# Projection stage of a cross-attention and feed-forward kernel: four re-orderings around the first two batches and the last

## The reference, cut to what matters

```python
# x, ctx: (8, 512, 512); mask: (8, 1, 512, 512); bias: (1, 16, 512, 512); 16 heads of 32
def attention(Q, K, V, mask, bias, ...):
    q = split_heads(Q @ Wq.T + bq); k = split_heads(K @ Wk.T + bk); v = split_heads(V @ Wv.T + bv)
    s = einsum('bhqd,bhkd->bhqk', q, k) / sqrt(32)
    s = where(mask == 0, -1e9, s) + bias
    return einsum('bhqk,bhkd->bhqd', softmax(s), v) @ Wo.T + bo
x = x + attention(layernorm(x), ctx, ctx, mask, bias, ...)
x = x + ffn(layernorm(x), W1, W2, ...)   # gelu(x W1^T) W2^T plus a routed low-rank part, width 2048
```

## Time and profile before

| | |
|---|---|
| median of 3 runs | 1793.49 us (1792.51 to 1795.33) |
| the profiled execution | 1790.85 us, span 1789.0 us |
| PE busy in the span | 1760.2 us (98%) |
| DVE, ACT, POOL busy | 1275.6 (71%), 912.1 (51%), 970.5 (54%) |
| mean granted TensorE clock | 0.997 of full speed |
| DMA in the first 7 of 40 slices | 330 to 356 GB/s, busy share 9 tenths or more |

### The profile page before, as it was taken

One profiled execution on the slowest core, in us unless ns is written; L12 is line 12 of the kernel. 1 busy time (PEld: TensorE's weight loads), 2 busy tenths in 40 slices (PEclk: granted clock), 3 DMA queues, 4 the chain that ended last, 5 costly groups with the idle time before them and its releaser, 6 DMA issues.

```text
span 1789.0 us, 33907 instructions
## 1 busy us (share of the span) xinstructions
PE 1760.2 (98%) x11842; PEld 1357.6 (76%) x11842; DVE 1275.6 (71%) x2866; ACT 912.1 (51%) x2038; POOL 970.5 (54%) x466
## 2 busy tenths in 40 slices
PE   8899998999999999999999999999999999999999
PEld 7788876555555555555778888888988889888888
DVE  8777788999999999999757555464654556645553
ACT  4323225999999999999434232312423224232231
POOL 1423347999999999998446343332342333423321
PEclk9999999999999999999999999999999999999999
DMA  9999999545436336340578684866948659577584
GB/s 330 330 346 341 343 356 336 180 143 189 143 99 233 113 125 226 106 131 19 171 239 301 226 291 141 317 198 188 320 131 299 208 187 320 157 263 239 163 280 144
DMA packets 213031, 396.90 MB, mean 222 GB/s; under 512 B 15232, under 2 KB 54784, under 8 KB 212352
## 3 DMA queue, kind: packets, MB, share of 16 engines
q1 hardware_dynamic: 209312, 381.62, 63.3%
q0 software_dynamic: 3264, 12.58, 2.0%
q10 hardware_dynamic: 288, 0.52, 0.1%
HBM read 319.17 MB, written 75.50 MB: 221 GB/s over the span
## 4 chain that ended last, share of the span: by engine, by line
PE 50%; DVE 2%; issue 0%; POOL 0%; ACT 0%; DVEq 0%; ACTq 0%
PE banks L2104 20%; PE banks L2078 17%; PE banks L1977 7%; PE banks L2016 5%; PE banks L1971 1%; DVE k_x L1532 0%; DVE k_x L1703 0%; DVE h_q L1693 0%; DVE n_w L1630 0%; DVE n_ru_l L1518 0%; DVE n_stats L1539 0%; DVE n_ru_l L1698 0%; DVE n_zo L1525 0%; DVE n_g_h L1710 0%; DVE n_sel L1638 0%
## 5 line engine op out<-in xcount | busy, mean ns | idle before, releaser
L2078 PEld LDWEIGHTS banks<-n_zo,n_w 128*128 128x128 f32 x2688 | 499.3, 188 | 66.8 <-DVE h_bias L1816 2.4
L2078 PE MATMUL banks<-n_zo,n_w 128*128 128x256 f32 x2688 | 532.5, 281 | 4.3 <-DVE h_bias L1816 2.2
L1461 POOL TENSOR_TENSOR n_g_l<-h_pos,n_g_h 128x512 fp32r<-128x512 f32 x128 | 196.3, 1533 | 559.4 <-DVE n_g_h L1710 559.4
L2104 PE MATMUL banks<-n_w,n_g_h 128*128 128x512 f32 x1024 | 383.2, 394 | 0.0
L1178 ACT ACTIVATE l_tiles<-l_tiles,l_small 128x512 f32<-128x512 f32 x376 | 267.4, 715 | 0.0
L1112 DVE CUSTOM_DVE_ANT_0 l_tiles<-banks,l_tiles 128x512 f32<-128x512 f32 x353 | 224.9, 687 | 24.7 <-PE banks L1014 23.9
L1025 PEld LDWEIGHTS banks<-ident,l_tiles 128*128 128x128 f32 x1524 | 164.8, 142 | 90.3 <-issue 71.8
L1025 PE MATMUL banks<-ident,l_tiles 128*128 128x128 f32 x1524 | 209.5, 281 | 0.7 <-ACT a_pT L1156 0.7
L2104 PE MATMUL banks<-n_w,n_g_l 128*128 128x512 f32 x512 | 201.7, 394 | 0.0
L2104 PEld LDWEIGHTS banks<-n_w,n_g_h 128*128 128x128 f32 x1024 | 193.0, 188 | 8.1
L1119 DVE COPY a_pT<-banks 128x512 f32<-128x512 f32 x256 | 164.6, 683 | 6.3 <-PE banks L1025 4.2
(11 more groups left out here) (263 smaller groups left out, 3523.9 us busy)
## 6 DMA issues: line engine op xcount, KB each, us to landing
n_w<-wf_d SPq DMA_DIRECT2D x448, 256.0 KB, 3.7
n_w<-w_d SPq DMA_DIRECT2D x112, 512.0 KB, 4.5
a_pos<-pos_d SPq DMA_DIRECT2D x16, 1024.0 KB, 5.6
l_bias<-in_bias POOLq DMA_DIRECT2D x9, 1024.0 KB, 7.9
l_tiles<-in_x SPq DMA_DIRECT2D x8, 1024.0 KB, 10.2
l_tiles<-in_xT SPq DMA_DIRECT2D x8, 1024.0 KB, 12.6
l_bias<-in_mask SPq DMA_DIRECT2D x8, 1024.0 KB, 14.3
k_d<-l_tiles SPq DMA_DIRECT2D x8, 1024.0 KB, 11.4
```

Of the source, the lines that this page charges most:

```text
L1461: pool.tensor_tensor(out=g_l[:, j % NG, :], in0=g_f[:, j % NG, :], in1=g_h[:, j % NG, :].bitcast(F32), op=ALU.subtract).then_inc(g_low, 1)
L2078: last = pe.matmul(bank, w1[:, q % NR, m, k * P:(k + 1) * P], zo[:, j, MOVING[i], k, :], start=s == 0 and i in (P1, P6, P5), stop=s == NPP ...
L2104: last = pe.matmul(ps_y[:, t, :], (g_h, g_l)[i][:, j % NG, t * P:(t + 1) * P], w2[:, j % NG, k, :], start=f == 0 and m == 0, stop=f == NF ...
```

## The change

Six edits, all in `project`. (1) ScalarE's first batch: the rounding of the four quarters of the value weights and the four key copies alternate, instead of four and four. (2) ScalarE: the rounding of the first W1 slice, `feed_high(0)`, leaves the end of batch 0 and stands in batch 1 behind `keep_row(1)`; the other slices stay where they were. (3) TensorE: from batch 1 on `R_HIGH` stands behind V0 instead of before it and `R_LOW` behind V1 instead of behind V0. (4) VectorE: from batch 1 on the first value addition is made behind the second diagonal, ahead of the mask, instead of with the other three. (5) VectorE, last batch: the order of scaling, masking and minima. (6) SP, last batch: values are stored by tiles, and one bias load goes between the second and the third.

```diff
@@ SP, body
+                for t in range(0 if more else NT):
+                    sp.wait_ge(bank_free, NPB + NVQ * b + t + 1)
+                    sp.dma_start(tokens(v_d[b])[:, t, :], v_s[:, t, :]).then_inc(v_out, 16)
+                    if t == 1:
+                        sp.wait_ge(min_done, B)
+                        sp.wait_ge(pos_out, 16 * (B + 1))
+                        load_bias(3)
@@ VectorE, body
                 diagonal(r_l)
+                if b > 0:
+                    values(b, 0, 1)
...
                 if b > 0:
-                    values(b, 0, NT)
+                    values(b, 1, NT)
...
+                else:
+                    scale_queries(b, 0)
+                    mask_queries(b, 0)
+                    first_minima(0)
+                    scale_queries(b, 1)
+                    scale_queries(b, 2)
+                    first_minima(1)
+                    mask_queries(b, 1)
+                    mask_queries(b, 2)
+                    scale_queries(b, 3)
+                    mask_queries(b, 3)
@@ ScalarE
+            def feed_high(b):
+                act.wait_ge(wf_in, 32 * (b + 1))
+                act.wait_ge(wf_out, 32 * (b + 1))
+                act.wait_ge(wo_out, 32)
+                for n, (ops, raw) in enumerate(f_parts):
+                    if n == 2:
+                        act.wait_ge(wf_summed, 4 * (b + 1))
+                    act.activation(f_h[:, ops, :], raw, ACT.Copy).then_inc(wf_high, 1)
...
                 for c in range(NC):
                     n = K_AT + c
+                    if b == 0:
+                        weight_high(0, c, c + 1)
                     act.wait_ge(projected, NPJ * b + n + 1)
...
                 else:
                     keep_row(b)
+                if b == 1:
+                    feed_high(0)
...
+                if b > 0:
+                    feed_high(b)
@@ TensorE, body
-                if b > 0:
-                    row_product(b, R_HIGH)
                 for t in range(NT):
...
-                    if b == 0 and t in (0, 2):
-                        row_product(b, R_LOW if t else R_HIGH)
+                    if t == 0:
+                        row_product(b, R_HIGH)
...
-                    if b > 0 and t == 0:
+                    if t == (1 if b else 2):
                         row_product(b, R_LOW)
```

More of the change, by code:

```diff
@@ L344, in body @@
                     load_ff(b)
+                for t in range(0 if more else NT):
[5 more added lines that the diff above has]
+                        load_bias(3)
                 sp.wait_ge(bank_free, NPB + NVQ * b + NT)
[L346 to L349, removed]
+                if more:
+                    sp.dma_start(tokens(v_d[b]), v_s[:, :, :]).then_inc(v_out, 16)
                 if more:
@@ L382, in _ @@
             sp.wait_ge(k_out, 16 * (B + 1))
-            sp.wait_ge(v_out, 16 * (B + 1))
+            sp.wait_ge(v_out, 16 * (B + NT))
         @block.gpsimd
@@ L600, in body @@
                         scale_queries(b, c)
-                for c in range(NC):
-                    if b > 0:
[L603 to L606, removed]
+                if more:
+                    for c in range(NC):
+                        if b > 0:
+                            scale_queries(b, c)
+                        mask_queries(b, c)
+                else:
[9 more added lines that the diff above has]
+                    mask_queries(b, 3)
             dve.wait_ge(piece_in[0], 32)
@@ L616, in _, with weight_high @@
         def _(act):
-            def weight_high(k):
+            def weight_high(k, first, end):
                 n, raw, loaded, _ = staging[k]
-                act.wait_ge(loaded, 16)
-                for c in range(NC):
+                if first == 0:
+                    act.wait_ge(loaded, 16)
+                for c in range(first, end):
                     if k == 1:
@@ L639, in body @@
             def body(b, more):
-                if b == 0:
-                    weight_high(0)
-                else:
+                if b > 0:
                     turned_high(b)
@@ L653, in body @@
                     keep_row(b)
+                if b == 1:
+                    feed_high(0)
                 if b == 0:
-                    weight_high(1)
+                    weight_high(1, 0, NC)
                     act.wait_ge(wo_in, 16)
```

## The result

The changed kernel takes 1797.12 us (median of 16 runs, 1795.62 to 1798.74) and the kernel before, run beside it, 1793.97. The ratio is 1.0017, with a 95% interval of 1.0009 to 1.0025: 3.1 us more, 1.6 to 4.5. That lies inside the forecast range, on the forecast side, but the size was forecast at 5.3. The interval does not reach 1; yet 0.17% is under the 0.2% that the prediction took for the least it could tell, so by its own split the outcome falls under "same", to which it gave 0.28, and not under "slower" with 0.60. One execution of the kernel before stands at 3429 us among those runs; the ratio leaves it out.

The account below looks back on a forecast made before the run. TensorE was busy 98% of the span, so only its pauses and slow stretches could be won. K0 of batch 2 1.7, clock 1.7 and stage end 1.9 sum to 5.3 us; added to the median 1793.49, 1798.8; range 1793.0 to 1802.0.

Parts of the forecast that it names:

- same: Outcome class for the whole kernel, no change beyond about 0.2%, 3.6 us; it holds Rival (b), chance 0.28.
- slower: Outcome class for the whole kernel: the forecast itself, 0.50, and Rival (c), 0.10; together 0.60.
- Edit 2 and SP: Batch 1: later rounding moves SP's release from 61.31 to 67.8; K0 of batch 2 starts at 85.5, 1.7 later.
- Rival (a): Batch 2's context arrives in time and the gain is kept: -4.0 us, 1789.5; chance 0.12.
- The pause: TensorE idles 7.6 us before K0 of batch 2, instead of 5.0 us a batch earlier.
- The clock: TensorE's slow clock behind the pause before batch 2 costs +1.7 us, bounds 0 and 3.4.
- Edit 1: Batch 0: alternating roundings and key copies delay VectorE; K0 of batch 1 0.8 later, at 44.3, bounds 0 and 1.8.
- Batch 7: Waits at two row products go, `FAC` is late next; queries and second scores come 0.4 us earlier.
- Rival (c): Batch 7: VectorE's mask comparison follows POOL's 4.61 us operation, `FAC` some 3 us later: 8.3 us, 1801.8; chance 0.10.
- The end: Last batch: SP's second query store leaves 1.9 us later, so the stage ends 1.9 later; upper bound 2.3.
- Rival (b): Mechanism holds, sizes smaller: end queue not full (-2.0 for +1.9) or clock returns at once; 1.4 us, 1794.9; chance 0.28.
- the 3.4 of batch 2: Before and in batch 2: K0 starting 1.7 us later plus 1.7 us for the slow clock behind the pause.

Follow-up runs that it names:

- SP's list was mended: Changed kernel with batch 2's context and x, the store of keys 1 and x transposed issued ahead of SP's wait for POOL: 1789.08 us, ratio 0.9974.

## Why the prediction was right, and where its size was off

**Edit 2 and SP.** Right. The release came at 67.67 (67.8 forecast), with two small errors that cancel: the row was copied 0.5 later than the 61.4 assumed, and POOL took 4.48, not 5.3. From release to K0 of batch 2 it was 17.82 us (17.7 forecast), and 17.8 in the four other variants that keep SP's order: this chain is a constant. K0 came at 85.49 (85.5). Rival (a), the context in time, was wrong for the changed kernel and true once SP's list was mended.

**The pause.** 5.92 us instead of 7.6. I let the products of batch 1 run from 55.3 to 77.9 without a wait. They ran from 55.79 to 79.42: 0.5 from K0 of batch 1 (44.83 instead of 44.3), and 0.85 at `FAC`, whose diagonals took 2.90 beside POOL's moved remainders. The 0.85 was in no term. It changes nothing in the sum, which goes by K0 of batch 2.

**The clock.** +1.7 forecast, +1.75 in the profile. But the size is not a constant: behind pauses of 4.3 to 5.9 us the keys of batch 2 took 12.4 to 13.6 instead of 10.9, so 1.5 to 2.7.

**Edit 1.** K0 of batch 1 stands at 44.8 on average over five profiles with it (44.25 to 45.11) and at 44.1 over seven without (43.54 to 45.20): 0.7, with 0.8 forecast, and a spread as large as the effect. No kernel shows it in a median.

**Batch 7.** The waits at the row products went and `FAC` became the next, as forecast: 278.12 is 3.05 later than in the earlier trace rows under a shift of 3.4, so 0.4 earlier than without the edits. Rival (c), the comparison behind POOL's operation, did not come.

**The end.** From the second scores on 2.3 was forecast (the 1.9 has the 0.4 of batch 7 taken off already); it was 2.4 by the profiles and 2.0 to 2.7 by the medians. Two errors met in it. The second store was forecast 4.0 behind the scores (its terms, 0.2 + 0.6 + 2.4 + 0.7, add up to 3.9) and left 4.57 behind them: I left out one wait, since the minima come so early now that they wait 0.54 for POOL's mask tile. And from that store to the next stage it took 7.09, where it took 7.46. Rival (b), a queue that is not full, fell: the last two stores took 4.17 against 4.56 in the earlier trace rows.

**The sum.** By the two profiles +1.66, +1.75 and the end's 2.4 less the 0.4 of batch 7 are 5.4, with 0.3 in the rounding and the rest: 5.7, against 5.3 forecast. The medians give 3.1, and 5.3 lies outside their interval. The changed kernel without edit 5 tells which terms were too large: by the forecast it should be 1.7 + 1.7 - 0.4 = 3.0 slower than the kernel before, and its medians give 0.4, interval -1.3 to 1.8. So the end's term holds, and the 3.4 of batch 2 are too much. The step that failed is their base: the kernel before was read from one execution, and 83.83 for K0 of batch 2 was taken as the old kernel's. That execution, with 1790.85, was the fastest of all of that kernel on record (the others took 1790.91 to 1796.50). Two experiments leave ScalarE's and POOL's order there as it was, and their rows show later times. POOL's first sum and the V0 of batch 1 with edit 5 alone:

```profile
54.20 0.74 POOL L421 TENSOR_TENSOR l_pos<-l_pos 128x256 f32<-128x256 f32 x1 [1.80 <-DMA l_pos<-in_W1T]
```

```profile
60.99 0.79 PE L764 MATMUL banks<-p_wv_h,p_cT_h 128*128 128x512 f32 x1 [5.70 <-ACT l_tiles L658]
```

and with edits 3, 4 and 6 alone:

```profile
54.58 0.73 POOL L426 TENSOR_TENSOR l_pos<-l_pos 128x256 f32<-128x256 f32 x1 [2.32 <-DMA l_pos<-in_W1T]
```

```profile
61.36 0.79 PE L761 MATMUL banks<-p_wv_h,p_cT_h 128*128 128x512 f32 x1 [6.43 <-ACT l_tiles L655]
```

In the profiled execution before, the W1 transfer landed over 1 us earlier, and V0 followed at 59.89:

```profile
53.06 0.75 POOL L421 TENSOR_TENSOR l_pos<-l_pos 128x256 f32<-128x256 f32 x1 [1.03 <-DMA l_pos<-in_W1T]
```

K0 of batch 2 was at 84.75 and 85.54 in the other two, 85.1 on average, not 83.83. Against that the changed kernel's 85.49 is only 0.3 later, and 0.3 + 1.75 + 2.4 - 0.4 = 4.1 is inside the interval. The changed kernel without edit 5 (K0 of batch 2 at 84.94, its keys 1.5 longer) comes to -0.2 + 1.5 - 0.4 = 0.9 against it, inside its own. That the two profiled executions agree with the forecast, 5.7 and 5.3, confirms no size: both are counted from the same old execution. The old kernel's pause hangs on when a transfer lands; the new one hangs on `R_LOW`, which does not wait for it. Three executions show this; how the rest of the old kernel's runs are spread in this place was not seen, so the last 1.0 us stays unassigned.

## What to carry to other kernels

When work moves to a later place on one engine, follow its last product to the queue that waits for it, and read what stands behind that wait on an in-order issuer: a wait worth nothing to anyone held back the next batch's context, and moving that one wait on SP turned a loss of 3 us into a gain of over 4, and of 8 with edits 1 and 5 left out. An operation shortened on an engine that shares with another is only worth what the other lets it keep. And before an effect of a few us is sized from one profile, see whether the stretch that it rests on hangs on a transfer's landing; if so, its times are one draw and not the kernel's.

## What the runs showed of the hardware that was not expected

In batch 2 TensorE's clock kept its upper level behind a pause of 1.86 us and fell behind those of 4.3 us and more, and what that cost was 1.5 and 2.7 us behind two pauses of 5.87, and 1.75 behind one of 5.92. Behind the pauses of 3.60 to 6.75 us ahead of the next stage it was 0.50 to 0.72 of full speed over the next 6 us in all twelve executions, the kernel before included. The third and fourth query stores together took 4.2 to 4.7 us to issue in every order tried, with one value store or four, though the second took 0.3 in each. VectorE's diagonals took 0.87, 1.38, 2.35, 2.90 or 3.96 for the same four operations, by what POOL did beside them.
